# Heads collected by ScalarE and normalised once for four units, in a two-layer attention and FFN kernel

## The reference

```python
y = softmax(q k^T * scale, causal) @ v            # layer 0, self ("s" in the kernel)
y = y + softmax(qc kc^T * scale) @ vc             # layer 0, cross ("x")
x = x + y @ Wp + bp
x = x + ffn0(layernorm(x))                        # weights in three values, rows in int8 steps
x = x + softmax(q k^T * scale) @ v @ Wo + bo      # layer 1, cross ("f"), q from layernorm(x)
x = x + ffn1(layernorm(x))
```

## Time and profile before

| | |
|---|---|
| median of 3 runs | 1823.12 us (1822.88 to 1827.1) |
| the profiled execution, its time | 1819.35 us |
| its span from first to last instruction | 1817.5 us |
| mean granted clock of TensorE | 0.952 of 2.4 GHz |
| TensorE, VectorE, ScalarE, GpSimd busy | 1618.0, 1389.3, 1147.5, 659.3 us |
| matmuls of the scores and the maxima | 543.4 and 525.9 us |
| VectorE's maxima of the x and f units | 651.0 us |

### The profile page before, as it was taken

How to read it: one execution, slowest core, us unless ns; L and a number is a source line. 1 busy time by engine, 2 the same in 40 slices (tenths; PEclk the granted TensorE clock), 3 DMA queues, 4 the chain that set the end, 5 groups by cost and what they waited for, 6 DMA issues and landing times.

```text
span 1817.5 us, 28822 instructions
## 1 busy us (share of the span) xinstructions
PE 1618.0 (89%) x9552; PEld 706.3 (39%) x9552; DVE 1389.3 (76%) x3221; ACT 1147.5 (63%) x2178; POOL 659.3 (36%) x918
## 2 busy tenths in 40 slices
PE   5898889998999989998999999988999997899677
PEld 1334334423443434433443344433443443333236
DVE  6678868788687787778787778878588787687287
ACT  1475485567765685667665685657655855765497
POOL 3436223551454134631454134623562242310140
PEclk7899889999999999999999999999999998999898
DMA  7444313323232323332242323332332232133113
GB/s 190 129 115 126 79 36 100 88 74 97 57 110 75 94 60 100 88 111 60 71 117 65 82 77 91 88 103 74 85 106 60 54 99 50 45 85 132 48 69 117
DMA packets 106949, 159.46 MB, mean 88 GB/s; under 512 B 20657, under 2 KB 83249, under 8 KB 106801
## 3 DMA queue, kind: packets, MB, share of 16 engines
q1 hardware_dynamic: 101904, 156.43, 30.9%
q10 hardware_dynamic: 4896, 1.18, 0.3%
HBM read 105.00 MB, written 51.38 MB: 86 GB/s over the span
## 4 chain that ended last, share of the span: by engine, by line
PE 56%; DVE 18%; ACT 12%; POOL 6%; issue 5%; DMA 2%; ACTq 1%; SPq 0%; DVEq 0%; POOLq 0%
PE acc L1511 12%; PE st L1497 11%; PE misc L1478 10%; PE misc L1454 7%; DVE nmax L1277 6%; PE misc L1426 4%; ACT probs L1003 4%; PE misc L1538 3%; PE misc L1466 3%; ACT tail_h L1073 2%; DVE misc L1271 2%; ACT hq L1032 2%; ACT tail_h L1058 1%; PE misc L1565 1%; PE misc L1552 1%
## 5 line engine op out<-in xcount | busy, mean ns | idle before, releaser
L1003 ACT ACTIVATE probs<-st 128x512 f32<-128x512 f32 (+3 forms) x1536 | 758.1, 552 | 373.7 <-PE st L1497 233.6
L1277 DVE TENSOR_REDUCE nmax<-misc 128x1 f32<-128x512 f32 x1024 | 651.0, 683 | 165.4 <-PE misc L1478 162.6
L1478 PE MATMUL misc<-stack 96*128 96x512 bf16 (+3 forms) x1536 | 525.9, 365 | 71.5 <-DVE nmax L1277 45.4
L1497 PE MATMUL st<-stack 99*128 99x512 bf16 (+3 forms) x1536 | 543.4, 364 | 42.2 <-ACT probs L1003 36.3
L1271 DVE CUSTOM_DVE_ANT_0 misc<-misc,mask_mx 128x384 f32<-128x384 f32 (+3 forms) x512 | 239.9, 517 | 99.4 <-PE misc L1478 95.0
L1497 PEld LDWEIGHTS st<-stack 99*128 99x128 bf16 x1536 | 149.3, 99 | 384.8 <-ACT probs L1003 231.6
L1478 PEld LDWEIGHTS misc<-stack 96*128 96x128 bf16 x1536 | 148.2, 100 | 222.2 <-DVE nmax L1277 85.6
L882 POOL TENSOR_TENSOR parts<-qk,zero 128x512 bf16<-128x512 f32 x78 | 81.5, 1044 | 216.3 <-ACT qk L986 216.3
L1511 PE MATMUL acc<-probs,v_x 128*32 128x512 f32 x1152 | 158.6, 623 | 0.0
L1511 PE MATMUL acc<-probs,v_s 128*32 128x512 f32 (+3 forms) x1152 | 117.1, 479 | 0.1
L1500 PE MATMUL st<-mask_st,identb 128*128 128x128 bf16 x512 | 112.7, 223 | 0.0
(11 more groups left out here) (264 smaller groups left out, 2098.9 us busy)
## 6 DMA issues: line engine op xcount, KB each, us to landing
parts_xk<-parts SPq DMA_DIRECT2D x54, 128.0 KB
parts_xq<-parts SPq DMA_DIRECT2D x54, 128.0 KB
stack<-parts_xq SPq DMA_DIRECT2D x36, 192.0 KB, 3.2
stack<-parts_xk SPq DMA_DIRECT2D x36, 192.0 KB, 3.6
parts_sk<-parts SPq DMA_DIRECT2D x48, 128.0 KB
parts_sq<-parts SPq DMA_DIRECT2D x48, 128.0 KB
stack<-parts_sq SPq DMA_DIRECT2D x32, 192.0 KB, 2.8
stack<-parts_sk SPq DMA_DIRECT2D x32, 192.0 KB, 3.5
```

The costliest lines, as they stand in the source:

```text
L1003: act.activation(probs[:, j % P_SLOTS, c, T - w:], st_bank(n, 4 * j + c)[:, 0:w], ACT.Exp, scale=SCALE).then_inc(exp_done, 1)
L1277: dve.tensor_reduce(nmax[:, ring, first:first + NT * (len(cs) - 1) + 1:NT], src, AX.X, ALU.max, negate=True).then_inc(misc_free[slot], 1)
L1478: last = pe.matmul(o, stack[0:ROWS, r, 0, c, P * i:P * i + P], stack[0:ROWS, r, 1, c, 0:w], start=True, stop=True)
L1497: last = pe.matmul(o[:, 0:w], stack[0:AUG, r, 1, c, P * j:P * j + P], stack[0:AUG, r, 0, c, T - w:T], start=True, stop=not causal)
```

## The change

The heads are no longer normalised unit by unit. ScalarE copies the 17 columns of each head from the misc bank into a new tile `raw` of 128 x 4 x 16 x 17 (its step `heads_out`, at the same place (1, 1)), waits until the copy is written, and frees the bank. When the fourth unit of an attention is in, a new step `normalise` at place (1, 2) does the rest once: VectorE takes one reciprocal of 64 sums, and GpSimd multiplies 1024 columns (`divide`). For the f units of the last batch VectorE does the product too. There is one `raw` and one `rsum`, so ScalarE waits for `normalised` before the first copy of the next four units. `y_T` waits for `normalised`. The Nones ahead of it are 10 instead of 6, and `mid_bias` stands behind `y_T`.

```diff
@@ unit_slot, close, layer0_end, turn
             if (j, c) == (1, 1) and prev:
                 out.append(("heads_out", prev))
+            if (j, c) == (1, 2) and prev and prev[2] == NU - 1:
+                out.append(("normalise", prev))
-    return [("mid_bias", b), ("y_T", b, "A"), None, None, ("residual", b, "A"), None]
+    return [None, ("y_T", b, "A"), ("mid_bias", b), None, None, ("residual", b, "A"), None]
-        start = slots(us[:5], [None] * 6 + [("y_T", b - 2, "C")] +
+        start = slots(us[:5], [None] * 10 + [("y_T", b - 2, "C")] +
...
+        def by_dve(s):
+            return s.unit[:2] == (B - 1, "f")
+        def divide(eng, s):
+            eng.tensor_tensor(y_of(s, s.unit[1])[:, :, :].rearrange("p t (h d) -> p t h d", d=D), raw[:, :, :, 0:D],
+                              rsum[:, :, :].unsqueeze(3).to_broadcast([P, NT, H, D]), ALU.mult).then_inc(normalised, 1)
@@ GpSimd
+            def normalise(s):
+                b, p, _ = s.unit
+                if by_dve(s):
+                    return
+                pool.wait_ge(rsum_done, s.n.base // NU + 1)
...
+                divide(pool, s)
             def y_T(s):
                 if s.args[0] == "A":
-                    wait_misc_read(pool, s, 0, ("heads_out", (s.key[1], "s", NU - 1)))
+                    pool.wait_ge(normalised, (AT[(s.key[1], "s", 0)]) // NU + 1)
@@ ScalarE
             def heads_copy(s):
                 act.wait_ge(values_done, s.n.times(4, VD + 4).at())
-                if s.n.base or s.i is not None:
-                    act.wait_ge(rsum_done, s.n.at())
                 act.copy(heads[:, :], acc[:, :]).then_inc(heads_full, 1)
+            def heads_out(s):
+                g, slot = s.unit[2], misc_slot(s)
+                wait_misc_full(act, s)
+                if g == 0 and s.n.base:
+                    act.wait_ge(normalised, s.n.base // NU)
+                act.copy(raw[:, :, HU * g:HU * g + HU, :],
+                         misc[slot][:, :].rearrange("p (t c r) -> p t c r", t=NT, c=HU)[:, :, :, 0:D + 1]).then_inc(raw_full, 1)
+                act.wait_ge(raw_full, s.n.base + 1)
+                act.sem_inc(misc_free[slot], 1)
@@ VectorE
-                dve.reciprocal(rsum[:, s.n.slot(4), :, :], o[:, :, :, D]).then_inc(rsum_done, 1)
-                dve.tensor_tensor(y_of(s, p)[:, :, HU * D * g:HU * D * (g + 1)].rearrange("p t (c d) -> p t c d", d=D),
-                                  o[:, :, :, 0:D], rsum[:, s.n.slot(4), :, :].unsqueeze(3).to_broadcast([P, NT, HU, D]),
-                                  ALU.mult).then_inc(misc_free[slot], 1)
+            def normalise(s):
+                kind = s.n.base // NU
+                dve.wait_ge(raw_full, s.n.base + 1)
+                if kind:
+                    dve.wait_ge(normalised, kind)
+                dve.reciprocal(rsum[:, :, :], raw[:, :, :, D]).then_inc(rsum_done, 1)
...
+                    divide(dve, s)
```

More of the change, by code:

```diff
@@ L175, in close @@
 def close(u):
-    return [("values", u, NT - 1), ("heads_copy", u), ("heads_out", u)]
+    return [("values", u, NT - 1), ("heads_copy", u), ("heads_out", u), ("normalise", u)]
 def warm_up(us):
@@ L262, in turn @@
     if b == 1:
-        start = slots(us[:1], [None] * 6 + layer0_end(0), 2) + \
+        start = slots(us[:1], [None] * 10 + layer0_end(0), 2) + \
             slots(us[1:5], layer0_ffn(0, [("v", 1, "s")]) + layer1_start(0), 2)
     else:
-        start = slots(us[:5], [None] * 6 + [("y_T", b - 2, "C")] +
+        start = slots(us[:5], [None] * 10 + [("y_T", b - 2, "C")] +
                       ffn_main(b - 1, [("residual", b - 2, "C"), ("v", b, "s")], layer1_last(b - 2)) + layer1_start(b - 1), b + 1)
@@ L282, in late_turns @@
     return [("load1", a), ("load0", c)] + \
-        slots(units(b, "x") + units(b, "s")[:1], [None] * 6 + [("y_T", a - 1, "C")] +
+        slots(units(b, "x") + units(b, "s")[:1], [None] * 10 + [("y_T", a - 1, "C")] +
               blend(ffn_main(a, [("residual", a - 1, "C"), ("v", b, "s")], layer1_last(a - 1)), tokens0(c) + project_qk(c, "x")) +
@@ L286, in late_turns @@
         slots(units(b, "s")[1:], [("load_mid", b)] + project_qk(c, "s") + layer1_norm(a) + [("v", a, "f"), None] + project_qk(a, "f"), B) + \
-        slots(units(c, "x")[:1], [None] * 6 + layer0_end(b) + [("load1", b)], B) + \
+        slots(units(c, "x")[:1], [None] * 10 + layer0_end(b) + [("load1", b)], B) + \
         slots(units(c, "x")[1:] + units(c, "s"), ffn_norm(b) + ffn_main(b, [("v", c, "s")]) + [("load_mid", c)] +
               layer1_norm(b) + [("v", b, "f"), None] + project_qk(b, "f"), B) + \
-        slots(units(a, "f")[:1], [None] * 6 + layer0_end(c) + [("load1", c)], B) + \
+        slots(units(a, "f")[:1], [None] * 10 + layer0_end(c) + [("load1", c)], B) + \
         slots(units(a, "f")[1:], ffn_norm(c) + [("ctx_T", c, "C")] + blend(ffn_main(c, [("v", c, "f")]), keys_c), B - 1) + \
@@ L295, in late_turns @@
               second[:9] + [("negmax_T", f[0])] + second[9:], B - 1) + \
-        slots(f[:1], [None] * 6 + layer1_end(b), B) + slots(f[1:], [], B) + close(f[-1]) + layer1_end(c)
+        slots(f[:1], [None] * 10 + layer1_end(b), B) + slots(f[1:], [], B) + close(f[-1]) + layer1_end(c)
 FIRST = turn_units(0)
@@ L511, in two_layers_kernel @@
         values_done = sem("values_done")
-        heads_full, rsum_done = sem("heads_full"), sem("rsum_done")
+        heads_full = sem("heads_full")
+        raw_full, rsum_done, normalised = sem("raw_full"), sem("rsum_done"), sem("normalised")
         negmax_split = sem("negmax_split")
@@ L900, in negmax @@
                 pool.tensor_tensor(part[2], nmax[:, r, :], part[1], ALU.subtract).then_inc(negmax_split, 1)
+            def normalise(s):
[3 more added lines that the diff above has]
+                pool.wait_ge(rsum_done, s.n.base // NU + 1)
+                if p == "x":
+                    pool.wait_ge(y_summed, b + 1)
+                if p == "s" and b:
+                    wait_misc_read(pool, s, KC - 1, ("y_T", b - 1, "A"))
+                if p == "f":
+                    wait_misc_read(pool, s, KC - 1, ("norm_T", b, "C"))
+                divide(pool, s)
             def y_T(s):
                 if s.args[0] == "A":
-                    wait_misc_read(pool, s, 0, ("heads_out", (s.key[1], "s", NU - 1)))
+                    pool.wait_ge(normalised, (AT[(s.key[1], "s", 0)]) // NU + 1)
                     pool.tensor_tensor(y["s"][:, :, :], y["s"][:, :, :], y["x"][:, :, :], ALU.add).then_inc(y_summed, 1)
@@ L1278, in maxima @@
                                   negate=True).then_inc(misc_free[slot], 1)
-            def heads_out(s):
-                _, p, g = s.unit
-                slot = misc_slot(s)
-                o = misc[slot][:, :].rearrange("p (t c r) -> p t c r", t=NT, c=HU)
-                wait_misc_full(dve, s)
-                dve.reciprocal(rsum[:, s.n.slot(4), :, :], o[:, :, :, D]).then_inc(rsum_done, 1)
-                if p == "x" and g == 0:
-                    dve.wait_ge(y_summed, s.b.at(1))
-                if s.unit == (B - 1, "f", 0):
+            def normalise(s):
[4 more added lines that the diff above has]
+                dve.reciprocal(rsum[:, :, :], raw[:, :, :, D]).then_inc(rsum_done, 1)
+                if by_dve(s):
                     dve.wait_ge(y_summed, B + 1)
-                dve.wait_ge(rsum_done, s.n.at(1))
-                dve.tensor_tensor(y_of(s, p)[:, :, HU * D * g:HU * D * (g + 1)].rearrange("p t (c d) -> p t c d", d=D),
-                                  o[:, :, :, 0:D], rsum[:, s.n.slot(4), :, :].unsqueeze(3).to_broadcast([P, NT, HU, D]),
-                                  ALU.mult).then_inc(misc_free[slot], 1)
+                    dve.wait_ge(rsum_done, kind + 1)
+                    divide(dve, s)
             def residual(s):
@@ L1314, in _ @@
             walk(dve, dict(consts=consts, consts_rest=consts_rest, project=project, split=split, w_peak=w_peak, w_row=w_row, w_tot=w_tot, w_ints=w_ints, stats=stats_, norm=norm, x_scale=x_scale, quant_x=quant_x, hidden=hidden,
-                           hid_peak=hid_peak, hid_scale=hid_scale, down=down, v=v, maxima=maxima, heads_out=heads_out,
+                           hid_peak=hid_peak, hid_scale=hid_scale, down=down, v=v, maxima=maxima, normalise=normalise,
                            residual=residual, finish=finish))
@@ L1524, in y_T @@
                 else:
-                    reads = [misc_read(s, 0, ("heads_out", (s.key[1], "f", NU - 1)))]
+                    pe.wait_ge(normalised, AT[(s.key[1], "f", 0)] // NU + 1)
                 y_ = y_of(s, "s" if k == "A" else "f")
```

9 lines of the change are left out of this document (5 added, 4 removed).

## The result

The changed kernel takes 1849.97 us (median of 4, 1840.39 to 1851.8), the kernel before 1823.18 (4 runs): ratio 1.0133, 95% interval 1.011 to 1.0156. So it is slower, by 26.8 us if the medians are taken, by 20 to 28 us if the interval of the ratio is. The forecast was 1835, +11.9: the direction holds, the size is about twice as large, and rival 2 (1851) names the time that came.

What follows compares the result with a forecast made beforehand. TensorE, busy 89% of the 1817.5 us span, was taken as the bound. Terms 10.4 + 1.4 + 1.5 + 4 + 6 - 10.9 = +12.4 us gave 1835.5 against the median, forecast as 1835, range 1811 to 1853.

Steps and rivals of the forecast that it cites:

- rival 2: Slower by more: GpSimd's product bars VectorE's splits for its whole length, waits for y grow; 1851 us, chance 0.2.
- waits for y of layer 0: TensorE waits 1.7 us instead of 0.4 for y_s in 8 batches: +10.4 us, bounds 5 and 29.
- waits for y of layer 1: TensorE's wait for layer 1's heads grows by 0.2 us, seven times: +1.4 us, bounds -5 and +17.
- the end: Last batch's f heads go serially through VectorE alone, with copy, longer reciprocal and 1024-column product: +1.5 us.
- ScalarE's copies: Two copies in each batch's units where ScalarE has no slack, half absorbed: +4 us, bounds 0 and 7.6, or 45.
- x product against the splits: GpSimd's product of the x heads holds VectorE's fq splits, 1.2 us in five batches: +6 us, bounds 0 and 12.
- VectorE's relief: VectorE loses about 52 us of work, shortening some 19 TensorE waits: -10.9 us, bounds 0 and 33.
- the steps' new order: Moved steps bring TensorE to y later, in layer 0 by 0.45 and 1.06 us; counted only within those waits.
- TensorE's clock: Mentioned under rival 2: longer waits may cost clock; more time at 1.2 GHz was not in the numbers.
- The chain behind s: Layer 0's reciprocal, GpSimd product (2.34 us) and sum in a row, leaving TensorE a wait of 1.7 us.
- rival 1: Faster: VectorE's relief counts wherever TensorE waits for it, -33 us, net -16; median 1807 us, chance 0.22.
- Busy times: VectorE's busy time falls to about 1338 us, ScalarE's rises to about 1186, GpSimd's to about 713.

Runs made afterwards that it cites:

- e1: Kernel before with only the changed order: 10 Nones instead of 6 at seven places, y_T ahead of mid_bias; 1819.37 us, ratio 0.9977.
- e7: e1 plus 96 ScalarE copies of 272 columns, with their own-write wait, from the tile of heads in SBUF; 1819.17 us, ratio 0.9985.
- e15: e11 with the end of layer 0 as in the kernel before (6 Nones, mid_bias ahead of y_T); 1858.57 us, ratio 1.0196.
- e17: e15 with y_T put ahead of mid_bias and nothing else changed; 1831.59 us, ratio 1.0049.
- e9: Changed kernel with the x heads' normalise step moved to place (3, 2) of the same first s unit; 1851.19 us, ratio 1.0155.
- e13: Changed kernel with the x heads' normalise step moved to the start of the second s unit, where no fq split stands; 1838.97 us, ratio 1.0086.
- e5: Changed kernel with all GpSimd products cut to one column per head (64 instead of 1024), output not the reference's; 1812.05 us, ratio 0.9947.
- e11: Changed kernel normalised unit by unit: 96 reciprocals of 16 sums on VectorE, 96 products of 256 columns on GpSimd; 1821.72 us, ratio 0.999.

## Why the prediction was right or wrong

| term | predicted | measured |
|---|---|---|
| waits for y of layer 0 | +10.4 | +9.0 in waits (+11.1 against e1); with the s products cut -20.5 |
| waits for y of layer 1 | +1.4 | -1.0 (2.9 for GpSimd's xn_C, 3.9 for VectorE's before); no run cuts the f products alone |
| the end | +1.5 | +1.5 (2.39 for 0.90) |
| ScalarE's copies | +4 | -0.2 to +1.4, bounds -2 and +5 (e7, from SBUF) |
| x product against the splits | +6 | +5.6 in waits; with it clear of the splits -11.0 |
| VectorE's relief | -10.9 | -7.1, the end's +1.5 in it, so about -8.6 |
| the steps' new order | none | -4 (e1) |
| other waits of TensorE | none | about +11: xn_C of the norm +5.5, nrow +3.5, exponentials +1.8 |
| TensorE's clock | none | +12.9 between the two profiled executions, about +6.5 by the means |

- **The step that failed** is the sentence "Longer waits may also cost clock ... and more of that isn't in my numbers". Every wait was priced at its own length, and nothing was set aside for what comes behind it. The two that I had put at 10.4 and 6 came as 9.0 and 5.6 us of waiting, right within 15%. But taking their causes away gave 20.5 and 11.0, together 15 us more than forecast, which is the distance between forecast and result. For x the excess is clock: with the product clear of the splits 7.5 us of TensorE's busy time go beside 5.7 us of waits, and the mean clock of all executions gives 6 to 7. For s it is clock only in part: of the 19.8 us 10.8 are the wait itself, about 5 are other waits, and about 4 are busy time (3 by the means). That the surplus of busy time is a lower granted clock is shown by the windows. That a wait brings it about is shown where one was taken away and the clock came back: for the second s unit, and for e15 against e17. For the fourth x unit it isn't. How the 15 us of the medians divide into clock and other waits stays open; in the two profiles it is 12.9 of clock and 5.2 of waits (17.6 for the 12.4 forecast).
- **The chain behind s** went as said: reciprocal, product and sum in a row, a wait of 1.43 where 1.7 was predicted. The product is 1.93 us, close to the lower of the two rows that I had (1.89), not the 2.34 that I took. The reciprocal of 64 sums takes 0.544 for my 0.5.
- **Rival 2** had the right time for half the right reason. Its first condition holds: the splits are barred for the product's length, at most 2.30 us, and e9 and e13 show it from both sides. Its second, a product over 2.6 us, didn't come. What filled its sum was the clock that it named and did not count, and small waits that it did not name; that it met the time to 1 us is luck.
- **ScalarE.** I charged 4 us for two copies in the units where it is busiest. e7 puts all 96 there at no cost that its noise lets me see; the forecast of 4 is its upper end.
- **VectorE's relief** came out near, 8.6 for 10.9 and far from the 33 of rival 1, but partly by luck: the waits for the maxima of x and f, which I had counted through for 10.9 us, fall by 2.8 between e7 and e5, and the rest of the gain is TensorE's busy time, 1622.1 to 1616.5. Of the 8.9 us by which these waits fell from the kernel before, 4.2 had gone with the order alone (41.2 in e1).
- **Busy times.** VectorE's came at 1357 for my 1338, half of it since held splits count as busy (1347.7 with the x product clear of them); ScalarE's 1183 for 1186, GpSimd's 704.5 for 713.
- **The new order** was costed as a part of the waits only. It gives 4 us by itself, so the new work costs 31 by the medians, not 27.

## What to carry to other kernels

Taking work from an engine with slack helps only where it holds up the bound engine; where what takes the work over stands in a chain, its length there counts in full, and where it doesn't (e13) it costs nothing that can be seen. Cut such a piece small and do it as its parts come in, so that one quarter stands at the end of the chain, not the whole; and look at what the new owner has in its queue, and which engine shares its memory port at that moment. And a wait of the matmul engine can cost more than its length: read the granted clock of the stretches behind such waits, over several executions, and add what it may take as the upper end of the term.

## What the runs showed of the hardware that I had not expected

- TensorE's clock took up to nearly half of a change's cost (12.9 of 30.5 us between the two profiles, 12.6 of 26.8 between e15 and e17). At waits of 1.4 us the unit around it kept a granted clock of 1.00, at 3.42 it had 0.93 and grew by 4.99, and behind waits of 2.23 and 0.52 the next unit had 0.80 and took 2.05 us longer. It is no function of the unit's own waits: one with 1.48 us of idle time had 0.91 in one kernel and 1.00 in another.
- The same program differs from execution to execution by its clock: 0.946 and 0.951 stood for 1849.9 and 1840.4 us, and 91 executions of the kernel before lay between 0.944 and 0.957.
- A GpSimd product of 1024 columns with one broadcast operand takes 1.93 us, the sum of two full operands 2.35; 256 columns take 0.62.
- VectorE's reciprocal costs by the column: 16 sums 245 ns in e11, 64 sums 544, so 6.2 ns for each more.
